# Marks and a tiles moved into the first 110 groups, one or two groups between TensorE's work and its answer, and a second buffer for the rows of marks

## The reference

```python
x_src = x[src]
x_dst = x[dst]
theta_x = (x_dst - x_src) @ theta_w.T + theta_b
phi_x = x_src @ phi_w.T + phi_b
e = relu(theta_x + phi_x)
out = segment_max(e, dst, num_segments=x.shape[0])
out = where(isfinite(out), out, 0.0)
return layernorm(x + out)
```

## Time and profile before

| | |
|---|---|
| three runs | 1243.34, 1245.99, 1250.09 us; median 1245.99 |
| profiled execution | 1242.66 us, its span 1240.8 us |
| POOL busy | 807.9 us, 65% |
| DVE, PE, ACT busy | 518.0, 313.0, 274.6 us |
| mean granted TensorE clock | 0.573 of full speed |
| HBM traffic | 198 GB/s over the span |

### The profile page before, as it was taken

The page is one execution under the profiler, slowest core; times in us unless marked ns, Lnnn a source line. Parts: engine busy times, 40 slices in busy tenths (PEclk is TensorE's granted clock), DMA queues, the critical chain, the costliest instruction groups (busy, mean ns, idle before and its releaser), DMA issues.

```text
span 1240.8 us, 5980 instructions
## 1 busy us (share of the span) xinstructions
PE 313.0 (25%) x953; PEld 194.2 (16%) x953; DVE 518.0 (42%) x1191; ACT 274.6 (22%) x568; POOL 807.9 (65%) x840
## 2 busy tenths in 40 slices
PE   6363322444342343110000000100014342430000
PEld 5142111222121232000000000000012131210000
DVE  4002332545343454543333433543325253537698
ACT  2022132233232232321111211321101010100144
POOL 6724756766666766677765676677746667667574
PEclk9667565666566655555555555555557565656555
DMA  8567545666465665676655665776547476747264
GB/s 262 164 196 225 178 156 169 229 204 210 159 204 181 215 213 194 231 241 201 199 191 166 209 192 191 256 228 206 192 139 261 145 236 225 240 136 229 100 195 157
DMA packets 111584, 245.76 MB, mean 198 GB/s; under 512 B 19141, under 2 KB 51226, under 8 KB 111546
## 3 DMA queue, kind: packets, MB, share of 16 engines
q0 software_dynamic: 39984, 109.21, 30.8%
q1 hardware_dynamic: 71130, 135.51, 29.9%
q10 hardware_dynamic: 432, 0.66, 0.2%
HBM read 129.89 MB, written 115.45 MB: 198 GB/s over the span
## 4 chain that ended last, share of the span: by engine, by line
DVE 29%; another core or an unknown queue 27%; issue 19%; POOL 10%; PE 6%; ACT 5%; DMA 4%; DVEq 1%; SPq 0%; ACTq 0%; POOLq 0%
DVE acc L582 16%; POOL rows L315 9%; DVE hist L582 6%; ACT hist L379 3%; DMA rows<-b_table,idx 2%; DVE stats L692 1%; PE acc L411 1%; DVE a_sb L681 1%; DVE hist L689 1%; DVE reached L596 1%; DVE a_sb L676 1%; PE ps_b L427 1%; PE ps_a L411 1%; DVEq L580 1%
## 5 line engine op out<-in xcount | busy, mean ns | idle before, releaser
L315 POOL DMA_INDIRECT rows<-b_table,idx x731 | 701.3, 959 | 372.2 <-issue 208.4
L379 ACT COPY hist<-acc 128x512 f32<-128x512 f32 x253 | 147.3, 587 | 471.0 <-DVE hist L582 241.3
L582 DVE SCALAR_TENSOR_TENSOR acc<-acc,reset,rows 128x256 f32<-128x256 f32 x253 | 124.7, 493 | 116.2 <-DVE acc L582 41.9
L582 DVE SCALAR_TENSOR_TENSOR acc<-hist,reset,rows 128x256 f32<-128x256 f32 x201 | 98.7, 491 | 151.5 <-issue 52.6
L582 DVE SCALAR_TENSOR_TENSOR hist<-acc,reset,rows 128x256 f32<-128x256 f32 x253 | 122.3, 483 | 80.8 <-DVE acc L582 41.0
L427 PE MATMUL ps_b<-diff_sb,conv_t 128*128 128x256 f32 x204 | 93.7, 607 | 223.5 <-issue 119.0
L447 PE MATMUL ps_d<-hi,row_of 128*128 128x512 bf16 x98 | 48.7, 497 | 381.3 <-remote 181.1
L462 PE MATMUL ps_a<-theta_sb,xt_sb 128*128 128x256 f32 x196 | 77.6, 545 | 130.6 <-issue 77.8
L427 PEld LDWEIGHTS ps_b<-diff_sb,conv_t 128*128 128x128 f32 x204 | 54.6, 295 | 243.0 <-issue 144.6
L582 DVE SCALAR_TENSOR_TENSOR acc<-hist,reset,early 128x256 f32<-128x256 f32 x51 | 25.2, 495 | 137.5 <-ACT hist L379 93.2
L384 ACT ACTIVATE signs<-ps_d,node_up 128x782 bf16<-128x782 f32 x49 | 44.7, 912 | 151.6 <-issue 74.6
(11 more groups left out here) (120 smaller groups left out, 342.9 us busy)
## 6 DMA issues: line engine op xcount, KB each, us to landing
runmax<-hist SPq DMA_DIRECT2D x260, 384.0 KB
rows<-b_table,idx POOLq DMA_INDIRECT x731
b_table<-rows SPq DMA_DIRECT2D x7, 896.0 KB
xt_sb<-in_xt SPq DMA_DIRECT2D x49, 128.0 KB
early<-in_x SPq DMA_DIRECT2D x12, 512.0 KB
out<-hist SPq DMA_DIRECT2D x11, 512.0 KB, 2.9
xt_sb<-in_xt SPq DMA_DIRECT2D x7, 512.0 KB
xt_sb<-in_xt SPq DMA_DIRECT2D x7, 384.0 KB
```

What stands on the lines that cost most here:

```text
L315: pool.indirect_dma_start(out=rows[:, PLACE[k], :], out_offset=None, in_=b_table, in_offset=bass.IndirectOffsetOnAxis(ap=idx[:, k:k + 1], ...
L379: nc.scalar.copy(hist[:, slot:slot + n - 1, :], acc[:, at:at + n - 1, :]).then_inc(s_copied, 1)
L582: nc.vector.scalar_tensor_tensor(new, former, reset[:, k:k + 1], row_at(k), ALU.min, ALU.max).then_inc(s_fold, 1)
```

## The change

Each kind of side work gets group numbers for each of its steps, so that an engine's answer stands one or two groups behind the work that it answers.

- Conversion e: transposes at group 2e, copy to `conv_t` and product at 2e + 1, copy of the product at 2e + 2.
- Mark t: VectorE and TensorE at group 5 + 2t, ScalarE's comparison at 7 + 2t. `EDGES_AT` and `ENDS_AT` become 106 and 110.
- Tile t of a: TensorE at 6 + 2t, VectorE's addition at 8 + 2t. SP loads the tile 11 ahead instead of 12.
- `row_of` has two buffers: VectorE waits for the mark two before, not the one before.

```diff
-    CONVERT_AT = {2 * e: e for e in range(EARLY)}
-    MARK_AT = {4 + 4 * t: t for t in range(NT)}
-    EDGES_AT, ENDS_AT = 4 + 4 * NT, 8 + 4 * NT
-    A_AT = {204 + t: t for t in range(NT)}
+    TURN_AT = {2 * e: e for e in range(EARLY)}
+    TURNED_AT = {2 * e + 1: e for e in range(EARLY)}
+    CONVERTED_AT = {2 * e + 2: e for e in range(EARLY)}
+    MARK_AT = {5 + 2 * t: t for t in range(NT)}
+    SIGN_AT = {7 + 2 * t: t for t in range(NT)}
+    EDGES_AT, ENDS_AT = 8 + 2 * NT, 12 + 2 * NT
+    A_AT = {6 + 2 * t: t for t in range(NT)}
+    A_READY_AT = {8 + 2 * t: t for t in range(NT)}
...
-        row_of = sb("row_of", [P, P], BF16)
+        row_of = sb("row_of", [P, 2, P], BF16)
...
-                if g in A_AT and A_AT[g] + 2 * CHUNK - 2 < NT and A_AT[g] >= 2:
-                    load_tile(A_AT[g] + 2 * CHUNK - 2)
+                if g in A_AT and 3 <= A_AT[g] < NT - 2 * CHUNK + 3:
+                    load_tile(A_AT[g] + 2 * CHUNK - 3)
...
+                if g in CONVERTED_AT:
+                    e = CONVERTED_AT[g]
+                    act.wait_ge(s_cb, e + 1)
+                    nc.scalar.copy(early[:, e, :], ps_b[:, 0, :]).then_inc(s_cbe, 1)
+                if g in TURNED_AT:
+                    e = TURNED_AT[g]
                     act.wait_ge(s_ct, e + 1)
                     nc.scalar.copy(conv_t[:].rearrange("p k n -> p (k n)"), ps_t[:, 0, :]).then_inc(s_cte, 1)
...
-                if g in MARK_AT:
-                    t = MARK_AT[g]
+                if g in SIGN_AT:
+                    t = SIGN_AT[g]
                     act.wait_ge(s_dstrow, t + 1)
...
-                    if t:
-                        dve.wait_ge(s_dstrow, t)
-                    nc.vector.scalar_tensor_tensor(row_of[:], cols_b[:], last_node[:, t:t + 1], reached[:], ALU.is_lt,
+                    if t >= 2:
+                        dve.wait_ge(s_dstrow, t - 1)
+                    nc.vector.scalar_tensor_tensor(row_of[:, t % 2, :], cols_b[:], last_node[:, t:t + 1], reached[:], ALU.is_lt,
                                                    ALU.mult).then_inc(s_rowof, 1)
...
-                if g in A_AT:
-                    t = A_AT[g]
+                if g in A_READY_AT:
+                    t = A_READY_AT[g]
                     dve.wait_ge(s_amm, t + 1)
```

More of the change, by code:

```diff
@@ L58, in build @@
     assert (NT - 1) % X_TILES == 0 and EMPTIED < min(X_AT) and max(X_AT) < NG
-    assert ENDS_AT < NG and max(A_AT) < NG and CONVERT_AT.keys() <= set(range(NG))
+    assert max(A_READY_AT) < LATE and max(SIGN_AT) < EDGES_AT and max(CONVERTED_AT) < LATE
     GATHERED = [k for k in range(STEPS) if k not in EARLY_OF]
@@ L419, in _ @@
             pe.wait_ge(s_xrows, 16 * EARLY)
-            def product(e):
-                pe.wait_ge(s_cte, e + 1)
-                if e:
-                    pe.wait_ge(s_cbe, e)
-                for k in range(KC):
-                    mm = pe.matmul(ps_b[:, 0, :], conv_t[:, k, :], diff_sb[:, k, :],
-                                   start=(k == 0), stop=(k == KC - 1))
-                mm.then_inc(s_cb, 1)
             for g in range(NG):
-                if g in CONVERT_AT:
-                    e = CONVERT_AT[g]
+                if g in TURN_AT:
+                    e = TURN_AT[g]
                     if e:
-                        product(e - 1)
+                        pe.wait_ge(s_cte, e)
                     for k in range(KC):
@@ L438, in _ @@
                     mm.then_inc(s_ct, 1)
-                if g == 2 * EARLY:
-                    product(EARLY - 1)
+                if g in TURNED_AT:
+                    e = TURNED_AT[g]
+                    pe.wait_ge(s_cte, e + 1)
+                    if e:
+                        pe.wait_ge(s_cbe, e)
+                    for k in range(KC):
+                        mm = pe.matmul(ps_b[:, 0, :], conv_t[:, k, :], diff_sb[:, k, :],
+                                       start=(k == 0), stop=(k == KC - 1))
+                    mm.then_inc(s_cb, 1)
                 if g in MARK_AT:
                     t = MARK_AT[g]
+                    mark = row_of[:, t % 2, :]
                     pe.wait_ge(s_rowof, t + 1)
@@ L446, in _ @@
                     for at, n in ((0, HALF), (HALF, STEPS - HALF)):
-                        pe.matmul(dst_rows[:, at:at + n], row_of[:], hi[:, at:at + n], start=True, stop=False)
-                        pe.matmul(dst_rows[:, at:at + n], row_of[:], lo[:, at:at + n], start=False, stop=True)
-                    pe.matmul(rows_of_nodes[:, t:t + 1], row_of[:], p_col[:], start=True,
+                        pe.matmul(dst_rows[:, at:at + n], mark, hi[:, at:at + n], start=True, stop=False)
+                        pe.matmul(dst_rows[:, at:at + n], mark, lo[:, at:at + n], start=False, stop=True)
+                    pe.matmul(rows_of_nodes[:, t:t + 1], mark, p_col[:], start=True,
                               stop=True).then_inc(s_dstrow, 1)
```

8 lines of the change are left out of this document (removed).

## The result

The changed kernel takes 1254.72 us (median of 20 runs, 1247.92 to 1264.55), the kernel before 1244.49 us beside it (20 runs, 1237.13 to 1254.48). The ratio is 1.0076, 95% interval 1.0047 to 1.0104: slower by 0.8%. The profiled execution of the changed kernel took 1252.56 us, its span is 1250.7 us, so 9.9 us over the span before.

What follows compares the result with a forecast made beforehand. GpSimd's queue of 731 gathers, 918 us, was taken as the bound, plus its lost waits. From 1242.7 us, minus 49 behind group 110, plus 29 before it, gave 1223 us, range 1180 to 1268.

Steps and rivals of the forecast that it cites:

- What bounds the kernel: Whole kernel: GpSimd's queue, 1.256 us a gather, 918 us for 731; other engines' idle time costs only where GpSimd waits.
- Behind group 110: Later stretch, with marks and a tiles moved out: GpSimd's loss falls from 63 to 14 us, gain 49 us (18 to 63).
- phases of 40 groups: Behind group 110: VectorE late in 81 of 142 groups, as two phases of 40, almost wholly hidden.
- the ring: GpSimd's 18 row slots: going from some 5 slots ahead to 18 hides VectorE's lateness for 38 groups, 16.3 us.
- VectorE late in every group: Rival, chance 0.10, behind group 110: by a lock or otherwise, loss 45 us instead of 14, time 1254 us.
- The rule on a lock: VectorE with two SBUF inputs and GpSimd block each other: groups behind 110 stay at 4.2 us, sum 1254; rejected by rows.
- Before group 110: First stretch, where the moved marks and a tiles arrive: loss rises from 57 to 86 us, cost 29 us (none to 60).
- The cycles: Before group 110: GpSimd's runs between restarts, 37.5 us each, shorten, so 11.1 cycles become 16.4 to 19.
- the loss of a cycle: Before group 110: GpSimd loses 5.1 us in each cycle, taken as unchanged by the change.
- the number of TensorE's instructions: Before group 110: 30 instead of 17 for a pair of groups, each 0.74 us in a late phase, 11 us a group.
- The smaller parts: Second buffer for rows of marks, SP's tile loads, and addition two groups behind its matmul: expected to give or cost nothing.
- The signs that were named: GpSimd's extra idle 5 to 25 us behind group 110, 80 to 100 before; group starts; TensorE busier, clock over 0.59.

Runs made afterwards that it cites:

- e1: Changed kernel with a tiles put back behind group 202, marks left early; ratio 0.9982 to the kernel before, on the first chip (before takes 1084.16 us).
- f1: The changed kernel itself again, on the second chip; ratio 1.0087 to the kernel before (1255.76 us there).
- g3: Changed kernel with one extra VectorE wait per group, on a semaphore long reached; ratio 1.0129 to the kernel before.
- f3: Changed kernel with four extra TensorE transposes, which nobody waits for, in each group from 112 to 252; ratio 1.0265 to the kernel before.
- g1: Changed kernel with one VectorE wait less per group, taken over by ScalarE two groups earlier; ratio 1.0114 to the kernel before.
- h4: Changed kernel with GpSimd waiting for folds only in every second group, for six slots at once; ratio 1.0236 to the kernel before.
- j1: f4 with four extra TensorE transposes, which nobody waits for, in each group from 4 to 109; ratio 1.0122 to the kernel before.
- j2: f4 with two extra TensorE transposes, which nobody waits for, in each group from 4 to 109; ratio 1.0067 to the kernel before.
- h2: Changed kernel with marks back in every fourth group, a tiles left early; ratio 0.9977 to the kernel before.
- f4: Kernel before with only the stages apart and the second buffer; marks in every fourth group, a tiles behind group 202; ratio 0.9984.

## Why the prediction was wrong

**What bounds the kernel: right, with a condition.** A gather costs 1.256 us of GpSimd's queue, and all else is loss. On the first chip the loss behind the first fold is nil (e1); on the others the kernel before takes 160 us more, of which 34 lie ahead of the first fold (110.9 us, against 76.8 in e1).

**Behind group 110: wrong, and this decides the sign.** The step was that only phases of 40 groups would be late, wholly hidden by the ring, with a loss of 14 us and a gain of 49. Measured, this stretch got 9 us shorter, and in f1 2.5 us longer: groups 110 to 159 gained 34 us (11 in f1), groups 160 to 252 lost 5, the last eight lost 21 (8 in f1). In the fourteen runs on the second to the fifth chip the stretch lies between 627.5 and 639.9 us, whatever stands there, beside 633.3 of the kernel before. With the side work gone the ticks don't come in phases of 40 groups, they last without a break to the end of the folds, from 700 us at the latest and in f1 and g3 from 550: groups 160 to 252 take 390.6 to 391.4 us, 4.20 us each, in the profile above, f1, f3, g1, g3 and h4, while every version that keeps marks, a tiles or pauses there shows breaks. The rival that says so, VectorE late in every group, had a chance of 0.10, a price of 45 us and a time of 1254; it is the one that came true, though in another form. That its 1254 meets the 1254.7 measured is luck: it has 9 us too much gain behind group 110 (18, measured 9) and 12 us too much cost before it. I let the ring hide 38 of its groups. That is about what f1, g1 and g3 show, where GpSimd keeps about 3.77 us a group until it is 14 or 15 slots ahead, between groups 150 and 160, and then waits for folds; in the profile above GpSimd was itself slowed to 4.2 us a group by longer gathers, and the ring stayed at 8 to 9 slots. The last eight groups, where each step has two dependent instructions, were taken as unchanged; they cost 20.6 us more in the profiled run.

That I read the earlier trace rows as phases that would stay phases was the error: the ticks break up only in versions with marks, a tiles or pauses there, which the change takes away.

The rule on a lock that was weighed there gave 1254 too. The lock is in the traces, but small, and it isn't what sets 4.2 us a group. Where a gather starts 0.12 to 0.32 us behind the start of a fold with two SBUF inputs, it ends 0.81 us after that fold's end, in the kernel before 46 times (8 us in all) and in e1 12 times (2 us); behind folds with one SBUF input, at the same distance, it takes 0.96 us at most in both. Where the gather starts first, as at 702.46 in e1 above, it keeps to 0.95 us too. One such pair in e1:

```profile
411.18 0.49 DVE L582 SCALAR_TENSOR_TENSOR acc<-hist,reset,rows 128x256 f32<-128x256 f32 x1 [3.44 <-DMA rows<-b_table,idx]
411.44 1.05 POOL L319 DMA_INDIRECT rows<-b_table,idx  x1 [0.31 <-issue]
```

The Trainium skill (SBUF — State Buffer, Who interferes with whom) states that a VectorE instruction with two SBUF inputs contends with a GpSimd instruction that reads SBUF. The traces agree, on both kinds of chip. But the lock lengthens gathers and not VectorE's gaps of 0.9 us, and the 1.24 and 1.10 us of the changed kernel are not its work: those gathers lie across folds that start 0.63 and 0.51 us into them, the first of which has one SBUF input, and they end on ticks. In f1, where GpSimd waits for VectorE anyway, the lock is there 127 times and makes its gathers 27 us longer in all.

**Before group 110: right in kind, too high in size.** Predicted +29 us, measured +17 in the profile and +19 in f1. The cycles came as forecast: 16 long waits of GpSimd where 10 were (16 to 19 cycles forecast, from 11.1), with 72 us lost, 76 in f1 (80 to 100 forecast). The term that was too high is the loss of a cycle, 4.5 us (4.8 in f1) instead of 5.1. (Two counts of the prediction are off and carry little: an unbroken stretch of GpSimd before is 27 gathers in the timeline behind the earlier trace rows, not 32, and 22 marks moved, not 23.) That the price hangs on the number of TensorE's instructions, whether or not anybody needs them, is what j1, j2 and the table above speak for. The traces count 632 more of them in this stretch (866 before, 1498 now); the 29 us would be 0.046 us each, the change shows 17/632 = 0.027, j1 0.020. h2 carries about as many as j2 and has the same first stretch, 414.9 us; its ratio is lower since its second stretch is shorter, 630.5 us against 634.8, and the rest was not traced to a place. By the ratios, marks and a tiles together cost more than the two apart. What makes them more than additive was not found.

**The smaller parts: right.** f4 shows the stages apart and the second buffer at nothing. The end moved by 1.3 us.

**The signs that were named.** Idle time beyond 0.30 us a gather behind group 110 came out at 5 us, as forecast, and proved nothing, for gathers got longer (in f1 it was 29 us, over the 25 forecast). Group 110 starts at 537.1 us (549 forecast), group 253 at 1110.7 us (1101 forecast). TensorE is busy 247.28 of the first 500 us at a clock of 0.71: both as forecast, but the kernel before meets this sign already, with 195.30 us at 0.63 in the same window, so it could not tell one theory from another.

**What stays open.** What makes the ticks, and why one chip has none. So the failed step is known, phases that would stay phases, and what came in their place; the cause behind it is not. The runs show that ticks hold instructions without a wait as well, that all engines share them, that they outlast GpSimd's last gather by 25 us, that pauses end them for a while, and that they don't follow the number of VectorE's instructions. Their phase is fixed in g1, g3 and h4 and drifts in f1, by some 0.6 us over 500 us. No run took a gather or a write of maxima away, so whether DMA traffic feeds them wasn't tried. And all times here come from executions whose instructions the profiler recorded; whether the recording itself takes part in the ticks wasn't tried either, so they are not shown to be there without it.

## What to carry to other kernels

Before moving work out of a stretch, ask what the stretch costs without it: here 279 dependent folds at 1.40 us are 390.6 us, more than the 385.6 us that they took with marks and a tiles among them. A row that gets cheaper in idle time is read together with the mean of its busy time, and with the stretch that follows the window. Instructions for which nobody waits were not free on the slower chips (j1: 1.2% for 848 of them); and on the first chip all four versions lay within 0.2% of the kernel before, so look at which regime a run is in first.

## What the runs showed of the hardware that was not expected

- The same kernel took 1084 us on one chip and 1244 to 1256 us on four others. In the slower regime starts fall on multiples of 0.700 us, for 460 us on end in the changed kernel's first profile and for some 600 us in f1 and g3, on VectorE, ScalarE, TensorE and SyncE alike, and long gathers of GpSimd end on them.
- A dependent fold of 0.49 us comes every 1.40 us on ticks, and 0.53 to 0.59 us after the last one off them (702.79, 703.32 and 703.91 in e1).
- TensorE's instructions without any wait start 0.70 to 1.40 us apart on ticks and 0.21 us for a whole transpose off them, in one and the same queue (f3).
- An indirect gather of GpSimd takes 0.95 us. It takes 1.10 and 1.24 us on ticks in the timeline around 900 us, and up to 1.20 us in e1 where it starts just behind the start of a fold with two SBUF inputs: it then ends 0.81 us after the fold.
- A TensorE instruction that nobody needs cost about 0.02 us of the whole.
